# A two-layer adaLN transformer kernel: order of the first sequence's key and query halves, placement of query parts, and the router logits kept on chip

## The reference, cut to what matters

```
h   = layernorm(x) * (1 + ca) + sa                     # modulation from silu(c) @ wmod
q   = (h @ Wq + bq) as 16 heads of 16                  # rotated (rope)
k,v = h @ Wk + bk, h @ Wv + bv                         # one head of 16, shared by all heads
att = softmax(causal(q k' / 4)); x += ga * ((att v) @ Wo + bo)
h   = layernorm(x) * (1 + cb) + sb
logits = h @ Wg + bg                                   # 16 experts
probs  = softmax(logits over the 512 tokens)
vals, idx = top_k(probs per expert, 64)                # then three matmuls per expert, scatter-add
```

## Time and profile before

| | us |
|---|---|
| median of 3 runs | 1191.42 |
| lowest, highest | 1188.30, 1193.76 |
| the profiled execution | 1191.18 |
| its span, first to last instruction | 1189.4 |
| PE busy | 1070.3 (90%) |
| DVE busy | 733.1 (62%) |
| ACT busy | 596.0 (50%) |
| POOL busy | 465.7 (39%) |
| PEld busy | 603.6 (51%) |

### The profile page before, as it was taken

One profiled execution on the slowest core, in us unless ns is written; L12 is line 12 of the kernel. 1 busy time (PEld: TensorE's weight loads), 2 busy tenths in 40 slices (PEclk: granted clock), 3 DMA queues, 4 the chain that ended last, 5 costly groups with the idle time before them and its releaser, 6 DMA issues. The chain is left out here.

```text
span 1189.4 us, 19798 instructions
## 1 busy us (share of the span) xinstructions
PE 1070.3 (90%) x6630; PEld 603.6 (51%) x6630; DVE 733.1 (62%) x1549; ACT 596.0 (50%) x1133; POOL 465.7 (39%) x692
## 2 busy tenths in 40 slices
PE   5499999999999998479999865999999998999996
PEld 3244554454454543346656432556666674455554
DVE  2667878787787783624333323767777781665665
ACT  3167677676766666013333324534444435866732
POOL 2444635444453511068888873333333310000000
PEclk9599999999999999579999987999999998999988
DMA  3522415233241411436676771011211002001001
GB/s 133 112 46 29 82 29 99 63 70 77 57 93 32 73 39 59 150 107 137 165 158 137 178 136 32 6 60 41 77 41 41 19 20 89 1 27 56 25 27 45
DMA packets 73685, 85.31 MB, mean 72 GB/s; under 512 B 12577, under 2 KB 67817, under 8 KB 73457
## 3 DMA queue, kind: packets, MB, share of 16 engines
q1 hardware_dynamic: 61296, 67.27, 21.6%
q0 software_dynamic: 12288, 16.79, 8.2%
HBM read 45.58 MB, written 25.47 MB: 60 GB/s over the span
## 5 line engine op out<-in xcount | busy, mean ns | idle before, releaser
L560 DVE TENSOR_REDUCE nmax<-psum 128x1 f32<-128x512 f32 (+3 forms) x352 | 215.6, 637 | 44.9 <-PE psum L779 39.7
L677 ACT ACTIVATE pT<-psum 128x512 f32<-128x512 f32 x320 | 181.1, 596 | 65.6 <-PE psum L800 35.6
L777 PE MATMUL psum<-k6T,q6T 96*128 96x512 bf16 (+3 forms) x512 | 128.2, 310 | 17.8 <-DVE nmax L560 14.0
L797 PE MATMUL psum<-q6T,k6T 99*128 99x512 bf16 x320 | 119.4, 382 | 1.1 <-ACT pT L677 0.9
L1085 POOL DMA_INDIRECT residual<-expert_y,idx_e x64 | 101.0, 1578 | 22.0 <-issue 16.5
L777 PEld LDWEIGHTS psum<-k6T,q6T 96*128 96x128 bf16 x512 | 45.7, 99 | 91.6 <-DVE nmax L560 59.1
L1604 DVE TENSOR_TENSOR l_scores<-psum,const_sb 128x512 f32<-128x512 f32 x128 | 79.5, 684 | 20.3 <-PE psum L1779 20.3
L779 PE MATMUL psum<-negs_bf,ident_bf 128*128 128x128 bf16 (+2 forms) x352 | 88.8, 252 | 0.0
L812 PE MATMUL psum<-pT,v 128*32 128x512 f32 x640 | 85.0, 604 | 0.0
L1072 POOL DMA_INDIRECT expert_tokens<-router_input,idx_e x64 | 62.7, 980 | 52.4 <-POOLq L903 33.2
L1737 PE MATMUL psum<-l_hT,l_w 128*128 128x512 f32 x128 | 63.7, 621 | 0.8 <-ACT l_plus_one L1681 0.8
(11 more groups left out here) (298 smaller groups left out, 2220.5 us busy)
## 6 DMA issues: line engine op xcount, KB each, us to landing
q6T<-q_parts SPq DMA_DIRECT2D x96, 128.0 KB, 4.5
expert_w<-in_ew SPq DMA_DIRECT2D x16, 768.0 KB, 4.8
x_in<-in_x SPq DMA_DIRECT2D x8, 512.0 KB, 4.3
residual<-x SPq DMA_DIRECT2D x32, 128.0 KB, 1.9
router_input<-h SPq DMA_DIRECT2D x32, 128.0 KB, 1.8
l_x<-residual SPq DMA_DIRECT2D x8, 512.0 KB, 4.3
x_dram<-l_x SPq DMA_DIRECT2D x32, 128.0 KB, 1.7
out<-c_out SPq DMA_DIRECT2D x16, 256.0 KB, 2.1
```

Source lines behind the costliest of these rows:

```text
L560: dve.tensor_reduce(nmax[:, i, u * nh:(u + 1) * nh], ps_s[:, n % SR, 0:nh * (i + 1) * P].rearrange("p (h k) -> p h k", h=nh), AX_X, ALU.ma ...
L677: act.activation(pT[:, n % PR].rearrange("p h t -> p (h t)"), ps_t[:, n % TR, :], ACT.Exp, scale=HD ** -0.5).then_inc(probs, 1)
L777: pe.matmul(out[:, a, :], q6T[0:6 * HD, b % 2, u * nh + a, i * P:(i + 1) * P], k6T[0:6 * HD, b % 2, 0:w], start=a == 0, stop=False, skip_g ...
L797: last = pe.matmul(out, k6T[:, b % 2, j * P:(j + 1) * P], q6T[:, b % 2, hg * 4:hg * 4 + 4, i * P:(i + 1) * P], start=True, stop=j < i)
```

## The change

Four things are changed, all in the attention block and at its seam to the routing:

1. In the list of the first sequence `kv` stands ahead of the second query half, and the first half's split ahead of `kv`: Q half 0, qd half 0, sp half 0, kv, Q half 1, rows, kT. On each engine only the order of kv and Q half 1 differs from before, as SyncE alone does `qd` and does no `sp`.
2. SyncE issues `load_rows` for the first sequence only at `rows`; those of the second and third come behind the second query half's parts of the first sequence.
3. In all sequences SyncE waits for each query part's own semaphore (`q_hi`, `q_mid`, `q_lo`) before the transfer that places it, in place of one wait for `q_lo` ahead of all six.
4. The logits go from `lg` to an on-chip tile `m.logits` (128 x 512, allocated over the whole kernel) in place of DRAM, and the routing uses that tile: its reload and VectorE's wait for it are gone. Of the last sequence's four pieces ScalarE issues two.

```diff
--- before.py
+++ after.py
@@ -147,6 +147,9 @@
 def attention_phase(nc, m):
     order = placed_order(ATTENTION_PLACE, ATTENTION_STEPS, attention_steps(), B)
     order.insert(order.index(("kT", 0)), ("rows", 0))
+    for first, later in ((("kv", 0), ("Q", 0, 1)), (("sp", 0, 0), ("kv", 0))):
+        order.remove(first)
+        order.insert(order.index(later), first)
     x_use, _ = index_of(order, ("hT", "kT", "mT", "oC", "h2T", "lg"))
     y_use, _ = index_of(order, ("kv", "Q", "oT", "pr"))
     s_use, _ = index_of(order, ("S",))
@@ -312,17 +315,19 @@
                         sp.wait_ge(rows_final, 1)
                         sp.dma_start(m.mod_rows[:, 0:4 * C], rows[:]).then_inc(rows_stored, 16)
                         sp.wait_ge(rows_stored, 16)
-                        for b in range(3):
-                            load_rows(b)
+                        load_rows(0)
                     if s[0] == "qd":
                         _, b, half = s
                         if b >= 2 and half == 0:
 
                             sp.wait_ge(t_fill, last_use(b - 2))
-                        sp.wait_ge(q_lo, 2 * b + half + 1)
                         for place, part in enumerate((0, 0, 0, 1, 1, 2)):
+                            sp.wait_ge((q_hi, q_mid, q_lo)[part], 2 * b + half + 1)
                             sp.dma_start(q6T[place * HD:(place + 1) * HD, b % 2, half * 8:half * 8 + 8, :],
                                          qs[:, half, part, :]).then_inc(q_placed[b % 2][half], 16)
+                        if b == 0 and half == 1:
+                            for later in range(1, 3):
+                                load_rows(later)
                     if s[0] == "mT":
                         _, b, i = s
                         sp.wait_ge(x_drain, x_use[s] + 1)
@@ -337,8 +342,9 @@
                     if s[0] == "lg":
                         b = s[1]
                         sp.wait_ge(x_drain, x_use[s] + 1)
-                        for i in range(NT):
-                            sp.dma_start(m.lg_d[b, :, i * P:(i + 1) * P], lg[32 * i:32 * i + E, b % 2, :]).then_inc(lg_store[b % 2], 16)
+                        for i in range(NT if b < B - 1 else 2):
+                            sp.dma_start(m.logits[b * E:(b + 1) * E, i * P:(i + 1) * P],
+                                         lg[32 * i:32 * i + E, b % 2, :]).then_inc(lg_store[b % 2], 16)
 
                 sp.dma_start(cT[:], m.d["cT"]).then_inc(c_loaded, 16)
                 sp.dma_start(x_in[:, 0], m.d["x"][0:NT].rearrange("i p c -> p i c")).then_inc(in_loaded[0], 16)
@@ -705,6 +711,11 @@
                         if b >= 2:
                             act.wait_ge(lg_store[b % 2], 16 * NT * (b // 2))
                         act.activation(lg[:, b % 2, :], ps_x[:, x_use[s] % XR, 0:P], ACT.Identity, bias=bg[:, 0:1]).then_inc(x_drain, 1)
+                        if b == B - 1:
+                            act.wait_ge(x_drain, x_use[s] + 1)
+                            for i in range(2, NT):
+                                act.dma_start(m.logits[b * E:(b + 1) * E, i * P:(i + 1) * P],
+                                              lg[32 * i:32 * i + E, b % 2, :]).then_inc(lg_store[b % 2], 16)
 
                 act.wait_ge(c_loaded, 16)
                 act.activation(eneg[:], cT[:], ACT.Exp, scale=-1.0).then_inc(exp_done, 1)
@@ -877,7 +888,7 @@
         def sem(name):
             return ctx.enter_context(nc.semaphore(name))
 
-        logits = sb("logits", [B * E, T])
+        logits = m.logits
         left = sb("route_left", [B * E, T])
         probs = sb("probs", [B * E, T])
         nmax = sb("route_nmax", [B * E, 1])
@@ -887,7 +898,6 @@
         vals = sb("route_vals", [B * E, 2, TOPK])
         idx = sb("route_idx", [B * E, TOPK], U32)
         idxf = sb("route_idxf", [B * E, 2, TOPK])
-        logits_in = sem("route_logits_loaded")
         loaded = sem("route_loaded")
         chain = sem("route_vector_steps")
         max_ready = sem("route_max_ready")
@@ -903,7 +913,6 @@
         with nc.Block() as block:
             @block.sync
             def _(sp):
-                sp.dma_start(logits[:], m.lg_d.rearrange("b e t -> (b e) t")).then_inc(logits_in, 16)
                 sp.dma_start(m.par_e[:, :, 4:7], m.d["eb"]).then_inc(loaded, 16)
                 sp.dma_start(wmod[:], m.d["wmod"][:, 1]).then_inc(mod_loaded, 16)
 
@@ -958,7 +967,6 @@
                     ins.then_inc(chain, 1)
                     dve.wait_ge(chain, count[0])
 
-                dve.wait_ge(logits_in, 16)
                 for r in range(TOPK // 8):
                     part = slice(8 * r, 8 * r + 8)
                     src = left if r else logits
@@ -2334,8 +2342,8 @@
         m.mod_rows = dram("mod_rows", (B, ROWS * C))
         m.x1_d = dram("residual", (B * NT, P, C))
         m.h2_d = dram("router_input", (B * NT, P, C))
-        m.lg_d = dram("router_logits", (B, E, T))
         m.x3_d = dram("x3_dram", (B * NT, P, C))
+        m.logits = sb("router_logits", [B * E, T])
         attention_phase(nc, m)
         m.cpl = coupling_lead(nc, m, ctx)
         with ExitStack() as outer:
```

## The result

The changed kernel took 1183.85 us in the median (six runs, 1180.45 to 1184.94); the kernel before took 1188.24 in the runs beside it. The ratio, taken over all these executions, is 0.9952, with an interval of 0.9934 to 0.9969: 5.7 us faster, between 3.7 and 7.8 (the two medians alone would give 0.9963). The forecast of the time was 1182.9, that of the gain 8.3 us. So the time lies in the range and the side is right, but the gain is 2.6 us short. That the time came within 1 us of the forecast is luck: the sum started from 1191.18, and the kernel before took 3 us less than that in these runs; from 1191.18 the ratio gives 1185.5, the upper end of the forecast's own range. A gain under 0.5% had been given a chance of 0.20. The profiled execution took 1184.94 us, with a span of 1183.1 against 1189.4.

A forecast was written before the change was run, and what follows sets the result against it. TensorE, 98% busy, bounds the attention, so only idle time at its two ends could be won: 1191.2 - 5.0 (start) - 3.3 (end) = 1182.9 us. Own range 1180.5 to 1185.5; with rivals and bounds 1179.0 to 1187.5.

The forecast's parts named there:

- key and first scores: Attention's start: key turned at 32.7 us, first scores at about 34.1, 3.1 us sooner; swap on TensorE costs nothing.
- The key's copy goes from in front of them to where it was idle, hence 35.8: VectorE at the attention's start: modulation rows end at 35.8 instead of 36.14 us, first maximum starts there, 1.9 us sooner.
- I take the middle, 6.1: Second sequence's input takes 6.1 us, between 8.0 and 4.2, landing at 45.15 instead of 50.19: 5.0 us gained.
- Rival (a): Second sequence's input isn't hindered by query parts: takes 4.2 us, gain capped at 6; 1181.9 us in all; chance 0.15.
- the first hole: TensorE's idle time at the attention's start, before 53 us: 5.0 us gained, bounds 3.2 and 7.0, capped at about 6.
- the seam: Last logits to routing: on-chip placement saves VectorE 3.85 us, of which 3.3 us counted; range 0.5 to 3.8.
- the matmuls are late next: Routing's start: modulation matmuls end at 500.0, after VectorE's tables at 499.5, so 3.3 us gained, 0.5 less than on VectorE.
- later sequences: Attention after 57 us: split query waits only bring SyncE's issues forward by some 3 us each; no time gained.
- (c): Gain at the start given back, as maxima or exponentials bound attention between 60 and 100 us; 1187.9 us; chance 0.08.
- (d): Slower: earlier query parts run beside small rows of maxima; at 0.7 us of TensorE per half, 1192.7 us; chance 0.02.
- the clock: TensorE's half clock around the attention's start: put at nothing, with at most 1.6 us gain or 1 us loss.

The follow-up runs named there:

- shortened: Changed kernel with GpSimd's multiply and add of the first sequence's second query half on 128 of 512 columns, rest uncomputed; one execution, 1183.05 us.
- one input: Changed kernel with GpSimd's multiply and add of the first sequence's second query half as full-width `tensor_scalar`, rotation left out; one execution, 1181.62 us.
- rows ahead: Changed kernel with the modulation rows moved ahead of the second query half; ratio 0.9918 to the kernel before.
- two parts: Changed kernel without the key ahead of the second query half and without a wait for each query part; ratio 0.9942 to the kernel before.
- input ahead: Changed kernel with the second sequence's input issued ahead of SyncE's wait for the modulation rows; ratio 0.9950 to the kernel before.
- seam on SyncE: Changed kernel with all four of the last sequence's logit pieces issued by SyncE, none by ScalarE; ratio 0.9978 to the kernel before.
- order alone: Kernel before with only the key moved ahead of the second query half; ratio 1.0018 to the kernel before.
- parts 2 to 4: Changed kernel with the key left behind the second query half, all else as changed; ratio 0.9965 to the kernel before.
- broadcasts alone: Kernel before with only six of the nine broadcasts moved behind the second query half's parts; ratio 0.9955 to the kernel before.
- both: Changed kernel with modulation rows ahead, second sequence's input ahead, and three of the last four logit pieces on ScalarE; ratio 0.9936 to the kernel before.
- seam alone: Kernel before with only the logits placed on chip, two last pieces on ScalarE and no reload; ratio 0.9979 to the kernel before.
- filled: Kernel "both" plus eight unread TensorE matmuls, six ahead of the first key's turning, two ahead of the second half's first scores; ratio 0.9904 to the kernel before.

## Why the prediction was right or wrong

**Right: key and first scores.** 32.67 and 34.12 against 32.7 and 34.1. The swap on TensorE cost nothing, as said, and the split waits bring the first half's parts forward (first issue 25.45 against 28.55). Two slips in this part of the working changed nothing: the rows are nine operations behind their copy, not eight, and ten maxima that start 1.9 us sooner end at 43.0, not at 42.6.

**Wrong: "VectorE is on the modulation rows until 36.14 ... The key's copy goes from in front of them to where it was idle, hence 35.8".** This step moved one operation of VectorE and left the others at the lengths that they had before. But those lengths belong to their neighbours: before, only 64-column operations of the key ran beside the rows; after, GpSimd's pair of 128x512 does. The price stood in the trace of before and I had not read it. Its timeline of GpSimd and VectorE, a few us ahead of the rows:

```profile
30.31 1.26 POOL L418 TENSOR_TENSOR q_turned<-q_product,q_swapped 128x512 f32<-128x512 f32 x1 [0.27 <-POOL q_swapped L415]
```

```profile
30.15 0.23 DVE L517 CAST negs_bf<-const_sb 128x128 bf16<-128x128 f32 x1
30.41 1.24 DVE L518 CAST negt_bf<-const_sb 128x128 bf16<-128x128 f32 x1
```

Two casts of one shape: the one that starts just ahead of GpSimd's operation takes 0.23 us, the one that starts 0.1 us behind its start takes 1.24. (The first cast of the three, at 29.56, took 0.56 us and not 0.22, beside the GpSimd operation ahead of that one.) Three such hits after the change (0.96, 0.96 and 0.92 us more than their kind) and 0.1 us on two smaller ones make 3.0 us; the copy of the rows started 1.0 us sooner than I had it, since the cast that was hit before isn't now; 35.8 + 3.0 - 1.0 gives the 37.8. The two kernels with the shortened and the one-input operations show the cause, the one with the rows ahead shows what the step was worth: at least 2.4 us at the scores.

The Trainium skill, "SBUF — State Buffer", section "SBUF: two separate sides", says that a pair of ports is an exclusive lock between GpSimd and those VectorE operations that run in a 2-port mode or have two inputs in SBUF, the latter only against a GpSimd operation that reads SBUF: who starts first has it for the whole instruction, the other blocks fully. The traces agree for GpSimd's operations with two inputs (VectorE ends 0.08 to 0.28 us after them). They do not for those with one, which read SBUF as well: beside the 1.54 us operation VectorE took 0.58 and, with two inputs of its own, 0.41. There the measurement decides.

**Wrong in size: "I take the middle, 6.1".** It took 6.7. The runs take the term apart: nine broadcasts ahead and the parts right behind, 8.0, 7.9 and 7.2; three ahead and the parts right behind, 6.6 to 6.9 in six kernels; three ahead and the parts 1.5 us behind, 5.6 at most, and 6.0 in the kernel with two parts. So of the 2 to 2.4 us that the input could win, about half comes from the broadcasts, and the other half part 3 gives away; with 0.8 us between executions of the same code neither half is known better than that. Rival (a) half fell by this: the parts do hinder the input, by about 0.9 us, but the 4.2 us that it took for the unhindered time were seen in no kernel, not even with nothing behind the input (6.0 with it ahead of everything). What makes up the rest stays open. I had written that split waits send the second half's parts forward and had costed it only at who waits for the parts, not at what lies beside them.

With both errors the first hole gave 2.55 us and not 5.0: the input issues 1.2 us sooner (42.15 to 40.95; six broadcasts fewer bring 2.8 us, the late rows take back 1.64) and takes 1.35 us less (8.0 to 6.7).

**Wrong in size: the seam.** The placement's issue (0.61 against 0.46) and landing (1.7 on SyncE, 1.9 on ScalarE, against 1.4) were both taken from the DRAM store, which had been the nearest row. From the last logits to the first maximum 2.4 us were gained instead of 3.85. Of the 1.5 us, some 0.8 are the longer issues, 0.4 a later start of SyncE's pieces, and 0.3 the landing. The further step, "the matmuls are late next", was not borne out: the modulation weights took 7.3 us from issue (480.48) to use, the matmuls ended at 498.29, and the transposes at 498.56 were released by VectorE. The two were ready 0.3 us apart, so the step cost nothing here. The load had taken 8.05 us before, and in the five kernels with part 4 where it takes 7.8 us or more (input ahead, shortened, one input, seam on SyncE, two parts) the transposes do stand right behind the matmuls, at 18.81 to 19.11 us from the first maximum in place of 18.72. So the step was sound and small, 0.1 to 0.4 us, and it was the load's length that hid it.

**Right: later sequences, rivals (c) and (d).** 98.27% busy from 100 to 200 us as before, 5.7 us of waits against 6.0; the shift at 53.6 us arrives at 475 us within 0.15 us. Nothing of it is given back by maxima or exponentials.

**Half right: the clock.** Put at nothing, with 1.6 of gain and 1 of loss as ends. In the changed kernel it is nothing. But over all runs the stretch from the second half's first scores to the last logits goes with when the clock comes back to full: 421.6 to 422.0 us where that is about 3 to 5 us behind those scores (before, changed, order alone, rows ahead, parts 2 to 4, shortened, one input, broadcasts alone), 422.9 where it is 9 us (two parts), and 423.8 to 424.6 where it is 11 to 12.5 us (input ahead, both, seam alone, seam on SyncE). It is no property of an edit: the seam alone has the first hole of the kernel before, the seam on SyncE that of the changed kernel, and each has the late clock once. The loss lies where the slow clock lies: between before and seam alone, which differ in no instruction there, the second half's first scores and the maxima that stand at 68.6 us in the kernel before are already 2.75 us further apart, and the next 370 us add nothing. What decides when the clock comes back is open. So up to 2.8 us are at stake in each execution, more than twice my bound of loss, and the filled kernel is the only one whose clock was held by design. How much of its 0.9904 is due to that stays open: the interval overlaps those of rows ahead and of both, and it was profiled once. By the trace it is 0.8 us ahead of "both" at the last logits, by the ratios 3.8 us.

**The sum.** 1191.2 - 2.55 + 0.15 - 2.37 = 1186.4 against the profiled executions' 1184.9, the rest being the 1.5 us of noise at the end; the gain by the runs' ratio, 5.7 us (3.7 to 7.8), is in keeping with the 4.8 of the three terms.

**What remains of the change.** Broadcasts (part 2) and placement (part 4) carry it. The key first (part 1) costs 1.3 us of the first hole at the statistics beside the other parts and about 2 alone (3 with TensorE late), unless the modulation rows go ahead of the second half too; the waits for each part (part 3) win nothing that anybody waits for without part 1, and cost about 1 us at the input. Three kernels have a lower ratio than the change (0.9952) and than parts 2 and 4 alone (0.9942): filled 0.9904, rows ahead 0.9918, both 0.9936; only the filled one's interval lies clear of the change's, and barely (0.9933 against 0.9934).

## What to carry to other kernels

When a step is moved, look at what its operations will run beside, not only at what waits for them: an operation on VectorE that takes 0.28 us took 1.24 beside a two-input operation of GpSimd, and the trace of before held such a pair. When a wait is split so that transfers start sooner, ask which transfer they now ride on; here it was the one that the hole waited for. And price a transfer by its target: the same 8 KB cost a third more to issue and 0.3 us more to land on chip than to DRAM. Last, hold a difference of under 1 us between two traces against two traces of the same code before giving it a cause: here the input alone differed by 0.8 us.

## What the hardware showed that I had not expected

- GpSimd's one-input operation of 128x512 (1.54 us) leaves VectorE's two-input operation at 0.41 us and takes a one-input one from 0.28 to 0.58; GpSimd's two-input operation holds either until it ends (1.24 to 1.37). Whether the inputs or the kind of operation make the difference is open.
- Placing 16 x 128 float32 into on-chip memory: 0.61 us of issue and 1.7 us to landing; to DRAM: 0.46 and 1.4. The Trainium skill, "DMA: Bandwidth & Descriptors", section "Anatomy of one DMA — SWDGE (gpsimd) path", written for transfers that GpSimd issues, calls the receipt of DRAM (HBM) the heaviest; for these, issued by SyncE and ScalarE, the on-chip landing took longer.
- Transfers issued behind an input lengthen it: 6.6 to 6.9 us with them 0.5 us behind (six kernels), 5.6 and 6.0 with them 1.5 us behind (two). The same page, section "Queues, rings and completion order", has descriptors consumed in ring order on each engine, from which the prediction concluded that they could not. But its sentence goes on that they carry no barrier and that a later one may finish its write before an earlier one, so it doesn't say what the prediction drew from it.
- The same program found its full clock at 59 us in one execution and at about 67 in another (before and seam alone, whose first 200 us are the same), and the stretch behind it was 2.8 us longer.
- TensorE's first full clock varies too: it comes at 19.3 to 21.7 us in eleven of the fourteen profiled executions and at 28.3 to 28.7 in three (order alone, rows ahead, filled). "Both" and rows ahead are in the same order up to there, and the rows' matmuls took 3.60 us and 6.32.
